# Third layer: fourteen units take the root on VectorE instead of ScalarE

## The reference

```python
log_ij = _logmap(x[:, None, :], x[None, :, :], c)      # arctanh(|sub|) * sub / |sub|, scaled
agg = jnp.einsum('ij,ijc->ic', adj / deg, log_ij)
```

## Time and profile before

| | |
|---|---|
| median of 3 runs | 1047.3 us (1044.82 to 1051.48) |
| profiled execution | 1044.31 us, span 1042.6 us |
| TensorE busy | 980.6 us (94%) |
| VectorE busy | 850.0 us (82%) |
| ScalarE busy | 750.8 us (72%) |
| GpSimd busy | 298.0 us (29%) |
| mean granted clock of TensorE | 0.981 |
| third layer's units | 529 to 954 us |

### The profile page before, as it was taken

The page is one execution under the profiler, slowest core; times in us unless marked ns, Lnnn a source line. Parts: engine busy times, 40 slices in busy tenths (PEclk is TensorE's granted clock), DMA queues, the critical chain, the costliest instruction groups (busy, mean ns, idle before and its releaser), DMA issues.

```text
span 1042.6 us, 16458 instructions
## 1 busy us (share of the span) xinstructions
PE 980.6 (94%) x6171; PEld 475.1 (46%) x6171; DVE 850.0 (82%) x1080; ACT 750.8 (72%) x805; POOL 298.0 (29%) x140
## 2 busy tenths in 40 slices
PE   6999979999899999999989999999999999998888
PEld 2444444446644444435434444444455454333455
DVE  6999969998678676697769987878878978888883
ACT  4655545554477667686788989988888888997683
POOL 1069980000001000004015464434343444342001
PEclk9999989999989999999998999999999999999999
DMA  9989987994048899788753444555655553446662
GB/s 330 420 332 422 423 366 241 345 403 162 1 160 282 292 304 301 262 268 303 261 188 127 160 127 158 170 194 164 198 163 162 165 171 116 155 142 201 214 217 78
DMA packets 96350, 238.43 MB, mean 229 GB/s; under 512 B 16401, under 2 KB 45073, under 8 KB 79889
## 3 DMA queue, kind: packets, MB, share of 16 engines
q1 hardware_dynamic: 87056, 220.62, 61.5%
q10 hardware_dynamic: 9216, 16.78, 4.2%
HBM read 219.55 MB, written 17.83 MB: 228 GB/s over the span
## 4 chain that ended last, share of the span: by engine, by line
PE 62%; DVE 20%; ACT 9%; issue 7%; POOL 1%; DMA 1%; DVEq 0%; SPq 0%; ACTq 0%; POOLq 0%
PE PS L577 39%; PE PS L756 9%; DVE TB L1559 6%; PE PS L896 4%; PE PS L865 4%; DVE work L2078 2%; ACT work L1268 2%; ACT work L1276 2%; DVE work L2066 2%; DVE ring L2084 1%; ACT work L1279 1%; DVE work L2072 1%; PE PS L589 1%; DVE work L1729 1%; ACT work L1262 1%
## 5 line engine op out<-in xcount | busy, mean ns | idle before, releaser
L555 POOL TENSOR_TENSOR ring<-work,ring 128x1024 f32<-128x1024 f32 x57 | 135.3, 2374 | 232.8 <-DVE work L2078 232.7
L1729 DVE TENSOR_TENSOR work<-work,ring 128x1024 f32<-128x1024 f32 x128 | 152.9, 1234 | 58.0 <-ACT work L1193 57.9
L1193 ACT ACTIVATE work<-PS,att_sc 128x1024 f32<-128x1024 f32 x128 | 148.0, 1201 | 68.5 <-PE PS L756 59.5
L1118 ACT ACTIVATE work<-PS 128x1024 uint8<-128x1024 f32 x128 | 124.2, 1024 | 100.0 <-PE PS L577 99.9
L577 PE MATMUL PS<-ring,work 128*65 128x256 f32 (+1 forms) x600 | 190.4, 465 | 3.8 <-DVE work L2105 3.8
L577 PE MATMUL PS<-work 128*64 128x512 f32 (+2 forms) x800 | 151.5, 519 | 1.4 <-ACT work L1262 1.2
L2072 DVE SCALAR_TENSOR_TENSOR work<-PS,work 128x1024 f32<-128x1024 f32 x72 | 88.0, 1222 | 55.0 <-PE PS L577 46.5
L756 PE MATMUL PS<-work 128*64 128x512 f16 x1024 | 124.0, 384 | 3.0 <-ACT work L1193 1.6
L577 PEld LDWEIGHTS PS<-ring,work 128*65 128x65 f32 x600 | 80.6, 138 | 90.7 <-issue 65.5
L1268 ACT ACTIVATE work<-work 128x1024 f32<-128x1024 f32 x72 | 76.0, 1055 | 34.8 <-DVE work L2066 34.7
L756 PEld LDWEIGHTS PS<-work 128*64 128x64 f16 x1024 | 59.0, 111 | 79.4 <-issue 34.7
(11 more groups left out here) (280 smaller groups left out, 1402.1 us busy)
## 6 DMA issues: line engine op xcount, KB each, us to landing
ring<-in_adj_t SPq DMA_DIRECT2D x96, 1024.0 KB, 5.4
ring<-in_adj_t SPq DMA_DIRECT2D x104, 512.0 KB, 4.1
work<-in_adj_t SPq DMA_DIRECT2D x32, 1024.0 KB, 8.6
codes<-work ACTq DMA_DIRECT2D x64, 256.0 KB, 7.2
ring<-codes SPq DMA_DIRECT2D x64, 256.0 KB, 4.6
H<-in_adj_t SPq DMA_DIRECT2D x24, 512.0 KB, 4.2
X<-in_x SPq DMA_DIRECT2D x2, 256.0 KB, 5.2
X<-in_x SPq DMA_DIRECT2D x1, 512.0 KB, 10.4
```

The costliest lines, as they stand in the source:

```text
L555: nc.gpsimd.tensor_tensor(near(n), sums(n), near(n), ALU.mult).then_inc(sem("near_ready"), 1)
L1118: nc.scalar.activation(made[:, k, u:HALF:2], PS[:, (4 + 2 * u) * BANK:(6 + 2 * u) * BANK], ACT.Relu).then_inc(sem("codes_made"), 1)
L1193: nc.scalar.activation(att[:, u, :], PS[:, (4 + 2 * u) * BANK:(6 + 2 * u) * BANK], ACT.Sigmoid, bias=att_sc[:, 2:3], scale=att_sc[:, 1:2]) ...
L1729: V.tensor_tensor(prob[:, m % 4, :], att[:, u, :], ring[:, s % RING, u * UNIT:(u + 1) * UNIT], ALU.mult)\
```

## The change

In the fourteen units without a mirror image other than 0 and 1, ScalarE no longer makes the root. VectorE multiplies the clipped square by the inverse root and writes the product into `sums(n)`, then adds as before. The waits for the buffer of `sums(n)` move to VectorE, VectorE's wait for the root becomes one for the inverse root, and the square of unit n+2 gets a wait for the sum of unit n, since the clipped square is now read later.

```diff
+def rooted(n):
+    return sum(mirrored(m) or m in (0, 1) for m in range(n + 1))
...
             def square2(n):
                 act.wait_ge(sem("z_ready"), n + 1)
+                if n >= ROT and rooted(n - ROT) == rooted(n - ROT - 1):
+                    act.wait_ge(sem("sum_ready"), n - ROT + 1)
...
                 act.wait_ge(sem("lnr_ready"), n + 1)
-                if 0 < n < ROTS:
-                    act.wait_ge(sem("agg1_done"), 4 * T - 2 + n)
-                if n >= ROTS:
-                    act.wait_ge(sem("near_ready"), n - ROTS + 1)
-                    if mirrored(n - ROTS):
-                        act.wait_ge(sem("mirror_ready"), mirrors(n - ROTS))
-                nc.scalar.activation(sums(n), lnr[:, n % ROT, :], ACT.Exp, scale=0.5).then_inc(sem("root_ready"), 1)
+                if rooted(n) > rooted(n - 1):
+                    if 0 < n < ROTS:
+                        act.wait_ge(sem("agg1_done"), 4 * T - 2 + n)
+                    if n >= ROTS:
+                        act.wait_ge(sem("near_ready"), n - ROTS + 1)
+                        if mirrored(n - ROTS):
+                            act.wait_ge(sem("mirror_ready"), mirrors(n - ROTS))
+                    nc.scalar.activation(sums(n), lnr[:, n % ROT, :], ACT.Exp, scale=0.5).then_inc(sem("root_ready"), 1)
...
             def sum2(n):
-                dve.wait_ge(sem("root_ready"), n + 1)
+                if rooted(n) > rooted(n - 1):
+                    dve.wait_ge(sem("root_ready"), rooted(n))
+                else:
+                    dve.wait_ge(sem("rin_ready"), n + 1)
+                    dve.wait_ge(sem("near_ready"), n - ROTS + 1)
+                    if mirrored(n - ROTS):
+                        dve.wait_ge(sem("mirror_ready"), mirrors(n - ROTS))
+                    link(V.tensor_tensor(sums(n), root[:, n % ROT, :], lnr[:, n % ROT, :], ALU.mult))
                 dve.wait_ge(sem("side_ready"), n + 1)
```

## The result

The changed kernel takes 1071.53 us in the median (1068.09 to 1077.29, 4 runs) against 1046.75 for the kernel before (4 runs), 24.8 more, a ratio of 1.0236 [1.0206, 1.0267]. Its profiled execution took 1071.2 with a span of 1069.3, so the spans stand 26.7 apart.

A forecast was written before the change was run, and what follows sets the result against it. TensorE was taken to bound units 20 to 57, gapless ScalarE the last of the fourteen. Terms 16.1 + 2.8 + 6.8 + 3.3 = 29.0 on the profiled 1044.3 gave 1073.3, stated as 1074 us; range 1060 to 1083.

The forecast's parts named there:

- Held product, 1.08 after GpSimd's: In the fourteen units, VectorE's new product ends 1.08 us after GpSimd's running product, wherever GpSimd started first.
- The period, 7.13: In a bare row of such units, each takes 4.79 + 2.34 = 7.13 us, against 4.85 before.
- Longer loop: Rival with nothing held up: units pay only the longer chain, 0.75 to 1.3 us each, +6.5, 1051 us; chance 0.07.
- The open place: Units 12, 58, 65 and 69: VectorE starts 0.17 us after GpSimd; GpSimd was taken to go first, no more than likely.
- The rival that had VectorE first in all four: Units 12, 58, 65 and 69: VectorE goes first, about 7 us less, +22, 1067 us; chance 0.24.
- The near tie of the earlier trace: VectorE, 0.02 us later, went first: its clipped square took an undisturbed 0.68 us, GpSimd's tiny instruction 0.75.
- The block in part that was put on unit 13: Unit 13's product only partly held, since node rows delay GpSimd's product of unit 12; sum 13 some 3.9 us late.
- The prediction's own sign: New products of about 2 to 2.7 us, sums 68 to 71 some 7 us apart, sum 71 27 to 30 later.
- The first rival's sign: GpSimd's product stretched to 3.5 us in units 12, 58, 65 and 69; that rival had chance 0.24.
- It passes to the end in full: Behind unit 71, the chain into the fourth layer has no transfer to hide the delay; 0 us added there.
- The last rival's mechanism: TensorE, half idle for 40 us at the end, is granted half its clock: some 2 to 10 us more; chance 0.07.
- the terms of 64 to 71 and 16 to 20: Predicted delays of +16.1 us in units 64 to 71 and +6.8 us in units 16 to 20.

The follow-up runs named there:

- e1: Changed kernel with VectorE's new product reading z from PSUM instead of the clipped square from SBUF: 1061.25 us, ratio 1.0125.
- e2: Changed kernel with GpSimd's product cut to 16 of 1024 columns in the units just before the fourteen: 1054.33 us, ratio 1.0061.
- e3: Changed kernel with GpSimd's product of the unit before each of the fourteen waiting for that unit's sum: 1075.12 us, ratio 1.027.
- e2b: Kernel before the change with GpSimd's product cut to 16 columns in the units just before the fourteen, a control: 1043.9 us, ratio 0.9962.
- e7: Changed kernel with tiny ScalarE copies delaying the inverse root in units 12, 58 and 65: 1075.31 us, one run.
- e4b: Changed kernel with 24 small unread TensorE products in the wait before the gather of unit 70: 1064.93 us, one run.
- e5: Changed kernel with the change kept in units 12 to 59 only; units 64 to 71 take their root from ScalarE: 1060.55 us, ratio 1.0128.

## Why the prediction was right, and where it was wrong

**Held product, 1.08 after GpSimd's: right.** 1.08 or 1.09 in all ten units where GpSimd went first (16 to 19, 59, 64, 68 to 71); taking away either the second SBUF operand (e1) or GpSimd's length (e2) gives 1.22. The Trainium skill (SBUF — State Buffer, SBUF: two separate sides) says the loser of the shared ports waits out the other's whole instruction, and that only a VectorE instruction with two SBUF inputs, or in its fast mode, can lose so to a GpSimd one. By e1, e2 and e3 the traces agree: nearly the whole instruction, 1.08 of 1.22 us, is left when GpSimd's ends, and the clipped square that e3 holds, with its one SBUF input, takes 0.68 us alone where the pair of the same size takes 1.22.

**The period, 7.13: right.** 7.12 and 7.11, and sum 69 lies 4.77 after pair 68, against the 4.79 that was worked out. So units 16 to 20 came out at 6.7 of the 6.8 predicted, with GpSimd first in all four of the fourteen among them, and the stretch of TensorE carried the delay unchanged.

**Longer loop: right.** Its share was worked out at 6.5 and measured at 6.1, or 7.4 against the control (e2, e2b).

**The open place: wrong in three of four.** This is the step that failed: "I take GpSimd at 0.17". VectorE went first in units 12, 58 and 65; only unit 69 went as forecast. The rival that had VectorE first in all four priced these three units at 2.1, 1.9 and 1.4 less, so 29.0 would have become 23.6; the layer measured 23.9 (units 12 to 15 kept 2.0 of the 3.3, 58 to 63 kept 0.7 of 2.8, 64 to 71 kept 14.4 of 16.1). The reason behind the choice was wrong as well: it compared the starts that the timeline shows, 0.17 apart, and weighed them against a lead-in of 0.14. e7 shows that the shown start is not the quantity, but how early the inverse root is ready. The near tie of the earlier trace rows pointed the right way and was overruled by an argument from the 0.14 that no row tested; there, too, the input had long been ready (the square ended at 605.17, GpSimd started at 606.32). The costs put on this place were right: with GpSimd first in unit 12 (e7) sums 12 and 13 come 2.9 and 3.8 late, worked out at 2.85 and 3.9, and units 12 to 15 and 64 to 71 cost 2.0 and 1.4 more than in the changed kernel, priced at 2.1 and 1.4. The block in part that was put on unit 13 did not happen, here or in e7: its product took 1.21, and GpSimd's product of unit 12 started after it, at 615.76. The prediction's own sign, sum 71 coming 27 to 30 later, did not come true: it came 23.8 later. The first rival's sign, GpSimd's product stretched to 3.5, did in three of the four places.

**"It passes to the end in full", with nothing added: wrong by 2.9.** The last rival's mechanism, priced at 2 to 10, happened beside the forecast and not in its place: with the longer wait ahead of the last gather TensorE's granted clock fell to 0.50, and filling that wait brought the clock and the 2.9 back (e4b, one run); all five executions with a wait of over 5 us lost there. The size is open: e7 lost only 0.9 with a wait of 7.76, and e5 2.3 with the old one.

The two errors have opposite signs, -5.1 in the layer and +2.9 behind it, so 26.8 came out near 29.0, and 1071.5 near 1074. Besides, the 29.0 were put on the profiled execution, 1044.3, which lies below the median of the runs; by the medians the change cost 24.8. The nearness of the total is partly luck; the terms of 64 to 71 and 16 to 20, four fifths of it, are not.

**A version that beats both** did not come up. Even with nothing held the product lengthens the layer by 6 us (e2), and the order that spares the product moves the hold to the next VectorE instruction (e3).

## What to carry to other kernels

Before moving elementwise work from a busy engine to VectorE, ask what GpSimd runs at that moment: a product of two SBUF operands that came behind the start of a GpSimd product took what was left of that product and about 1.1 us more (1.22 alone), and one operand taken from PSUM avoided it. Ask also whether the moved work is parallel to the loop or in it; here 0.97 us left ScalarE per unit and 1.26 entered the only path that ScalarE waits for. To forecast who wins a near tie compare when the inputs are ready, not when the instructions are shown to start. Look, too, at the granted clock behind a wait that grows on TensorE: here it went with a loss of 0.9 to 3.0 us.

## What the runs showed of the hardware that was not expected

- VectorE, shown to start 0.16 to 0.17 us after GpSimd, still went first when its last input had been ready 0.08, 0.11, 0.16 or 0.36 us before GpSimd's start; GpSimd then took 3.61 or 3.62 instead of 2.36. With the input 0.01 before or up to 0.04 after, VectorE was held for 3.26 to 3.35. The Trainium skill's section named above says that whichever starts first has the ports; by the starts shown in the profile the traces do not agree.
- A clipped square with a single SBUF input was held by GpSimd in six units of the kernel before, not only in that of the earlier trace rows, and for up to 2.04 us instead of 0.68 in e3. Each time it ended 0.55 after GpSimd's product, where the held two-input product ended 1.08 after it.
- The same wait of 2.53 us ahead of the last gather was followed by a granted clock of 1.00 in one execution (the kernel before) and of 0.57 in another (e5).
